# Last cross attention: values and turned probabilities with one batch on each half of the partitions

## What is computed

```python
q = (x @ w_q).reshape(B, Sq, HEADS, DIM_HEAD).transpose(0, 2, 1, 3)
k = (context @ w_k).reshape(B, Skv, HEADS, DIM_HEAD).transpose(0, 2, 1, 3)
v = (context @ w_v).reshape(B, Skv, HEADS, DIM_HEAD).transpose(0, 2, 1, 3)
sim = jnp.einsum('bhid,bhjd->bhij', q, k) * SCALE
attn = jax.nn.softmax(sim, axis=-1)
out = jnp.einsum('bhij,bhjd->bhid', attn, v)
out = out.transpose(0, 2, 1, 3).reshape(B, Sq, INNER)
return out @ w_o + b_o
```

## Time and profile before

| | us |
|---|---|
| Median of 3 runs | 1196.51 (1196.50 to 1196.58) |
| The profiled execution | 1195.89 |
| Its span, first to last instruction | 1194.2 |
| TensorE busy | 785.8 |
| VectorE busy | 755.2 |
| ScalarE busy | 405.2 |
| GpSimd busy | 397.9 |

### The profile page before, as it was taken

The page is one execution under the profiler, slowest core; times in us unless marked ns, Lnnn a source line. Parts: engine busy times, 40 slices in busy tenths (PEclk is TensorE's granted clock), DMA queues, the critical chain, the costliest instruction groups (busy, mean ns, idle before and its releaser), DMA issues. The chain is left out here.

```text
span 1194.2 us, 21152 instructions
## 1 busy us (share of the span) xinstructions
PE 785.8 (66%) x7623; PEld 576.9 (48%) x7633; DVE 755.2 (63%) x2348; ACT 405.2 (34%) x755; POOL 397.9 (33%) x517
## 2 busy tenths in 40 slices
PE   4884587467776868634489916545899999932232
PEld 2653343345554765432279804423578778720111
DVE  4997486686777144555558765675536556558985
ACT  3896531322222203212123222133344444422221
POOL 3444899143344210024624400000012122113553
PEclk9998798555555658855589955766979999975555
DMA  8400000011000005001164320000000000000000
GB/s 294 167 2 2 0 1 1 16 54 56 20 1 1 2 1 88 1 0 52 47 200 159 129 77 1 1 1 0 1 2 2 2 3 2 2 1 0 10 9 18
DMA packets 23418, 42.53 MB, mean 36 GB/s; under 512 B 2658, under 2 KB 13507, under 8 KB 22580
## 3 DMA queue, kind: packets, MB, share of 16 engines
q1 hardware_dynamic: 21044, 36.50, 9.4%
q0 software_dynamic: 2272, 4.69, 1.2%
HBM read 22.56 MB, written 8.40 MB: 26 GB/s over the span
## 5 line engine op out<-in xcount | busy, mean ns | idle before, releaser
L3002 POOL TENSOR_TENSOR l3x_probs<-l3x_E,l3x_inv 128x1024 f32<-128x1024 f32 x16 | 30.9, 1934 | 103.2 <-DVE l3x_inv L3041 103.2
L362 ACT ACT_TABLE_LOAD x9 | 11.5, 1283 | 144.2 <-PEq L151 144.2
L3027 DVE TENSOR_REDUCE l3x_top<-l3x_p_s 128x8 f32<-128x512 f32 x32 | 20.6, 686 | 59.5 <-PE l3x_p_s L2873 59.5
L2016 POOL DMA_INDIRECT moe_replies<-l1gb_inbox x39 | 38.6, 990 | 57.4 <-DVE l1gb_inbox L2151 52.9
L2105 ACT ACTIVATE l1gb_hidden<-l1gb_hidden 128x512 f32<-128x512 f32 x39 | 24.6, 630 | 72.1 <-DVE l1gb_hidden L2137 67.6
L2062 PE MATMUL l1gb_p_h<-l1gb_xT,l1gb_w_now 128*128 128x128 f32 x312 | 44.6, 288 | 6.3 <-issue 4.7
L673 POOL TENSOR_TENSOR l0x_kspread<-l0x_kT,l0x_groupmask 128x512 f32<-128x512 f32 x32 | 32.7, 1044 | 47.5 <-ACT l0x_kT L600 47.5
L917 PE MATMUL l0f_p_h<-l0f_hpad,l0f_taps 128*128 128x512 f32 x96 | 47.0, 639 | 0.0
L3364 PE MATMUL l3fb_p_h<-identity_bf,l3fb_hq 128*128 128x128 bf16 x64 | 8.3, 311 | 55.6 <-DVE l3fb_hq L3302 55.6
L2062 PEld LDWEIGHTS l1gb_p_h<-l1gb_xT,l1gb_w_now 128*128 128x128 f32 x312 | 39.5, 198 | 10.4 <-issue 8.9
L1171 PE MATMUL l1a_p_scores<-l1a_kspread,l1a_qT 128*64 128x256 f32 x64 | 17.5, 638 | 38.5 <-POOL l1a_kspread L1344 38.1
(11 more groups left out here) (658 smaller groups left out, 2533.6 us busy)
## 6 DMA issues: line engine op xcount, KB each, us to landing
l1gb_w_now<-params_l1w SPq DMA_DIRECT2D x39, 256.0 KB, 2.3
params_l1w<-in_l1w SPq DMA_DIRECT2D x2, 2048.0 KB, 12.0
l_toeplitz<-s4d_lags SPq DMA_DIRECT2D x64, 64.0 KB
moe_slots<-l1f_blank SPq DMA_DIRECT2D x1, 2535.0 KB, 16.1
l1gb_inbox<-moe_slots SPq DMA_DIRECT2D x9, 260.0 KB, 5.1
params_l3x<-in_l3x SPq DMA_DIRECT2D x1, 2048.0 KB, 22.6
l1g_rows<-moe_replies SPq DMA_DIRECT2D x8, 256.0 KB, 5.1
params_l2x<-in_l2x SPq DMA_DIRECT2D x1, 1028.5 KB, 16.0
```

Source lines behind the costliest of these rows:

```text
L2016: pool.indirect_dma_start(moe.replies[:, :], bass.IndirectOffsetOnAxis(inbox[:, j, D:D + 1].bitcast(I32), 0), outbox[:, j, :], None).then_ ...
L3002: pool.tensor_tensor(Pn[:], E[:], wide(inv[:].rearrange("p a j -> p j a").unsqueeze(3), [P, J, 2, S]), ALU.mult)\
```

## The change

The values are computed with the batch on the partition halves, both heads of a pair side by side: two matmuls of 128 weights. The probabilities are turned in 64x64 tiles, by matmuls against the 64x64 blocks of the identity, so that the turned ones have the batch on the partition halves as well. Heads then contracts over the half b and writes into the half a; the order of its loops is the same. All results of a tile now have the same order of heads, so one matrix Wo serves, with 128 weights a matmul, and the copy with swapped halves is gone, with its two transfers, its semaphore and its wait. VectorE's copy to oT reorders: it writes runs of 64 elements.

```diff
-        oT = s.sb("oT", [P, 2, J, S])
+        oT = s.sb("oT", [P, J, P])
...
-        wo = [w("Wo"), core.swapped_wo[:]]
...
-                pe.wait_ge(core.swapped_wo_loaded, 32)
...
-                    for b in range(2):
-                        for a in range(2):
-                            last = pe.matmul(p_o[a * S:(a + 1) * S, b, :, :], core.ctxT[0:DC, t * P + b * S:t * P + (b + 1) * S],
-                                             wv[:, a, :], start=True, stop=True)
+                    for a in range(2):
+                        last = pe.matmul(p_o[:, a, :, :], core.ctxT[0:DC, t * P:(t + 1) * P], wv[:, a, :], start=True, stop=True)
...
-                            last = pe.transpose(p_t[:, j, :], Pn[:, j, :, :].rearrange("p a k -> p (a k)"), core.ident[:])
+                            for a in range(2):
+                                for b in range(2):
+                                    rows = slice(b * S, (b + 1) * S)
+                                    last = pe.matmul(p_t[rows, j, a * S:(a + 1) * S], Pn[rows, j, a, :], core.ident[rows, rows],
+                                                     start=True, stop=True)
...
-                                rows, half = slice(a * S, (a + 1) * S), a ^ b
-                                last = pe.matmul(p_o[half * S:(half + 1) * S, b, j, :], v[rows, b, j, :],
-                                                 PT[rows, j, b * S:(b + 1) * S], start=True, stop=True)
+                                rows = slice(b * S, (b + 1) * S)
+                                last = pe.matmul(p_o[a * DH:(a + 1) * DH, b, j, :], v[rows, a, j, :],
+                                                 PT[rows, j, a * S:(a + 1) * S], start=True, stop=True)
...
-                        for b in range(2):
-                            last = pe.matmul(p_t[b * S:(b + 1) * S, 0, :], oT[:, b, j, :], wo[b][:, j * D:(j + 1) * D],
-                                             start=(j == 0), stop=(j == J - 1))
+                        last = pe.matmul(p_t[:, 0, :], oT[:, j, :], w("Wo")[:, j * D:(j + 1) * D], start=(j == 0), stop=(j == J - 1))
...
-                    dve.tensor_copy(oT[:], p_o[:]).then_inc(oT_ready, 1)
+                    dve.tensor_copy(oT[:].rearrange("p j (b s) -> p b j s", s=S), p_o[:]).then_inc(oT_ready, 1)
```

More of the change, by code:

```diff
@@ L87, in __init__ @@
         self.out_bias = {name: self.sb(f"out_bias_{name}", [P, D]) for name in ("l0_bo", "l3_bo")}
-        self.swapped_wo = self.sb("l3x_swapped_wo", [P, 1024])
         self.value_weights = self.sb("l0x_value_weights", [DC + 1, D])
@@ L116, in __init__ @@
         self.out_bias_loaded = self.sem("out_bias_loaded")
-        self.swapped_wo_loaded = self.sem("swapped_wo_loaded")
         self.value_weights_loaded = self.sem("value_weights_loaded")
@@ L254, in later_loads @@
     sp.dma_start(core.text_mask[:], d["text_mask"].partition_broadcast(P)).then_inc(core.masks_loaded, 16)
[L255 to L258, removed]
 class Named:
```

## The result

The changed kernel takes 1209.01 us (median of 4, 1207.43 to 1209.94) against 1196.55 us of the kernel before, run beside it: ratio 1.010, 95% interval 1.0082 to 1.0117. It is slower by about 1%, as forecast, and 2.0 us above the predicted time.

A forecast was written before the change was run, and what follows sets the result against it. TensorE was taken to bound the last cross attention; a tile grows from 11.27 to 11.93 us, 14 x 0.66 = 9.2 plus 1.3 at the end gives +10.5, so 1206.4 profiled and 1207.0 median, range 1203 to 1212.

The forecast's parts named there:

- The round of 0.059: Turn of the probabilities: two diagonal tiles take 0.059 us a round, as four do in heads; 32 rounds plus 0.15 give 2.03.
- 0.10 for each side of a switch of shape: TensorE, between blocks of different tile shape: each side of a switch costs 0.10 us, read from keys 1.88 and queries 1.98.
- halving the number of matmuls in values and output: TensorE: buys almost nothing, as the halves already ran in pairs; values 1.82 for 1.87, output 1.88 for 1.90.
- heads against the convolution: Price of the turn's round: 0.059 us as in heads (2.03), or 0.111 as in the convolution (3.70, 1233.8 us), chance 0.07.
- The rival of the rate of issue: Turn on TensorE: 64 records cost 1.09 us on any tiles, a tile changes by -0.28, time 1192.0; chance 0.05.
- the block of scores at half clock: First scores block at granted clock 0.50 loads in 1.80 us instead of 1.02; taken as evidence that the array's clock sets a round.
- The rival of the strided copy: VectorE's copy to oT: runs of 64 double it to 2.45 us, values wait 0.71 a tile, time 1217; chance 0.03.
- The add's wait: Inside the turn: TensorE's 0.3 us a tile wait for VectorE's add (L3058) goes under the longer turn.
- The two rules that spoke for the slow turn: Skill rules on row tiles sharing a PSUM bank and on weight loads overlapping only across row groups; they support 0.111 a round.
- The count and the ends: Last cross attention: 14 full tiles at +0.66 give 9.2 us, the end from tile 14 on +1.3, together +10.5.
- Dropped loads: Two early 256 KB transfers from SyncE: taken as worth nothing, between nothing and a 4.2 us gain, since no engine waits.
- the bounds of the round: Turn's round between 0.052 us (1203.5 us in all) and 0.068 us (1211.6 us in all), which set the range.

The follow-up runs named there:

- e4: The changed kernel with full 128x128 transposes as before and the halves exchanged in the scores; 1193.55 us, ratio 0.9967 to the kernel before.
- e6_strided_weights: The changed kernel with probabilities laid out so the turn reads its weights with a step of 128 elements; 1238.16 us, ratio 1.034.
- e3_scores_diagonal: The kernel of e4 with the scores on the two diagonal tiles alone instead of all four; 1209.16 us, ratio 1.0086.
- e1: The changed kernel with the two dropped transfers, their tile, semaphore and wait put back, the tile unused; 1208.48 us, ratio 1.008.
- e8: The kernel of e2 once more, in more rounds; 1197.50 us, ratio 0.9997.
- e2: The kernel before with the two transfers issued in the second feed-forward stage instead of the first stage; 1195.91 us, ratio 0.9985.
- e5: The kernel before, unchanged, profiled and timed again; 1198.02 us, ratio 1.0002.
- e9: The kernel of e4 with VectorE's add moved between its two subtractions of the maximum, except in the last tile; 1195.31 us, ratio 0.9966.
- e11: The kernel of e4 once more, unchanged; 1194.48 us, ratio 0.9971.

## Why the prediction came out as it did

The prediction was right in sign, in mechanism and in nearly every term.

**The bound.** TensorE set the pace before (10.94 of 11 us) and after (11.00 of 11), so its added work landed in the stage one for one: 0.65 a tile where 0.66 stood.

**The terms.** Slots from start to start, in us:

| | forecast | measured |
|---|---|---|
| queries | 1.88 | 1.89 |
| values | 1.82 | 1.81 |
| scores | 1.09 | 1.09 |
| turned input | 0.16 | 0.17 |
| output | 1.88 | 1.87 |
| turned probabilities | 2.03 | 2.01 |
| keys | 1.98 | 1.98 |
| heads | 1.09 | 1.10 |
| tile | 11.93 | 11.92 |

The round of 0.059 was read from heads; the turn's 64 loads span 1.94, and (1.94 - 0.13)/31 = 0.058. The 0.10 for each side of a switch of shape came out in queries and keys, and in the output it shows once more in e4, where no switch follows, as 0.08: 1.79 for 1.87. That halving the number of matmuls in values and output would buy almost nothing was right too: 0.06 and 0.03.

**The choice that decided** was heads against the convolution, 2.03 against 3.70 for the turn. It was made because of the step in the convolution's weights, and e6_strided_weights bears that reason out: with that step the turn takes 3.70 on the same tiles.

**The rival of the rate of issue** falls with e3_scores_diagonal, 2.01 for 64 records on two tiles. The forecast's row against it, the block of scores at half clock, does not decide alone: a rate that all tiles share, set by the array's clock, would have slowed there as well, and left the turn near 1.09. **The rival of the strided copy** falls with its 1.22. The add's wait went under the longer turn as said, and no new wait came.

**The two rules that spoke for the slow turn.** The scores of e4_swap_in_scores write one bank from both row halves, in different partitions, where those of the kernel before write two banks; both take 1.09. The Trainium skill, TensorEngine Tiling (Array Packing), Restrictions and Gotchas, says that row tiles can't access one bank at the same time; these rows disagree where the partitions differ. And a turn whose two row halves each reload their one tile 32 times keeps 0.058 a round, below the 135 ns of a single load. The Trainium skill, TensorE: Matmul & The Clock Gate, Part 3, says that a load overlaps matmuls in flight only where the row group differs; by these rows loads also overlap with the work of their own row group.

**The count and the ends.** Up to the turn of tile 14 the stage grew from 178.26 to 187.58, by 9.32 where 14 x 0.66 = 9.2 stood; from there on from 13.00 to 14.42, by 1.42 where 1.3 stood.

**Off TensorE.** Dropped loads taken at nothing: e1 and e8 agree, and e2 alone had left it open.

**What missed** is the step from the span to the median. I added 10.5 to the profiled execution's 1195.89 and 0.62 for the median. The stage was 10.74, but the profiled execution of the changed kernel also began the stage 2.80 later, and the median stands 2.0 above the forecast. The working had no term for what the same kernel does ahead of the stage from one execution to the next; e5 and the pair of e2 and e8 show 2.7 and 4.5 us of it. Three runs of before that agreed within 0.08 us hid it: beside the experiments the same kernel had medians from 1197.56 to 1198.57. Against 19 of those runs, with a median of 1198.03, e1, whose last cross attention takes 202.01 us as the changed kernel's does, is 10.45 us slower, which is the forecast's 10.5. That the range of 1203 to 1212 held the time owes something to luck: its width came from the bounds of the round, and this scatter was not in it.

## What to carry to other kernels

Count f32 records by the tile they run on: where four 64x64 tiles are in use 64 records took 1.09 us, where only the two on the diagonal are 2.01, so a product that always stays in its own half paid nearly double. Three ways to bring the halves together were run: two matrices Wo in the kernel before, the turn in small tiles in the changed one, and scores that write the half a ^ b in e4. The last was the cheapest: those scores run on all four tiles anyway and took no longer, the full transposes and the single output matrix stay, and the kernel came out 0.3% below the kernel before and 1.3% below the changed one. And before a few microseconds are explained, profile the unchanged kernel a second time and compare the stage itself, not the total.

## What the hardware did that was not expected

- The same kernel began this stage at 863.65 and at 868.11 us in two executions (e2, e8). Some 640 us ahead of it the first feed-forward stage took about 102.4, 105.0 or 107.9 us, with nothing between in 13 profiles and whatever the kernel, at a granted clock of 0.95, 0.92 or 0.89 over 64 us of it.
- The loop that was made 0.29 us a tile shorter was followed, in all three profiles, by blocks at the 1.2 GHz level: 3.97 us won in the loop, 3.2 lost behind it in e9, with the same instructions in the same order that ran at 1.00 in e11.
- A step of 128 elements in the weights makes a load of 64x64 f32 last 202 ns instead of 135, but a round of two tiles 0.111 us instead of 0.058: the round nearly doubles where the load grows by half.
